# Token sums of a gated mixture layer computed in pieces during the attention, first two quads interleaved with the last attention batch

## The reference, cut to what matters

```
x = x + tanh(g_xattn) * attention(layernorm(x), ctx)       # 8 batches of 256 tokens, D = 512
h = layernorm(x)                                            # 2048 tokens
w_e  = top-8 of softmax(h @ gate_w.T), zeros elsewhere      # 64 experts
flat = w_e[:, inv_map]                                      # 8 groups of 8
soft = softmax over each group where flat != 0
scalar = flat.sum(-1)                                       # one per token and group
xg = h + soft @ mask_up[g]                                  # for each group g
a  = silu(xg @ gate[g].T) * (xg @ up[g].T)                  # 352 inner rows
x  = x + tanh(g_ffn) * sum_g scalar_g * (a @ down[g].T)
```

## Time and profile before

| What | Value |
|---|---|
| Median of 3 runs | 1113.91 us (1113.6 to 1114.71) |
| The profiled execution | 1112.23 us |
| Its span, first to last instruction | 1110.4 us |
| Mean granted TensorE clock | 0.983 |
| TensorE busy | 1056.9 us, 5388 matmuls |
| VectorE, ACT, GpSimd busy | 764.2, 376.9, 615.2 us |
| HBM read, written | 70.67 MB, 23.27 MB |

### The profile page before, as it was taken

One profiled execution on the slowest core, in us unless ns is written; L12 is line 12 of the kernel. 1 busy time (PEld: TensorE's weight loads), 2 busy tenths in 40 slices (PEclk: granted clock), 3 DMA queues, 4 the chain that ended last, 5 costly groups with the idle time before them and its releaser, 6 DMA issues.

```text
span 1110.4 us, 14594 instructions
## 1 busy us (share of the span) xinstructions
PE 1056.9 (95%) x5388; PEld 899.3 (81%) x5388; DVE 764.2 (69%) x1328; ACT 376.9 (34%) x635; POOL 615.2 (55%) x479
## 2 busy tenths in 40 slices
PE   8999999999977799989999999969999999999997
PEld 7988998998865677878888888858888888888885
DVE  7775666666588768797788787876656665666554
ACT  5333333333332344334234333333233333332331
POOL 1212201210344757765787876777777777777761
PEclk9999999999998899999999999989999999999999
DMA  9112213323682421113111211472222202221202
GB/s 331 59 39 95 63 61 86 82 79 48 125 264 102 89 65 54 64 43 66 53 64 44 71 65 62 141 228 93 99 72 71 71 28 71 72 71 46 71 27 76
DMA packets 86861, 94.75 MB, mean 85 GB/s; under 512 B 20240, under 2 KB 71184, under 8 KB 86800
## 3 DMA queue, kind: packets, MB, share of 16 engines
q1 hardware_dynamic: 86432, 93.80, 28.1%
q10 hardware_dynamic: 368, 0.15, 0.1%
HBM read 70.67 MB, written 23.27 MB: 85 GB/s over the span
## 4 chain that ended last, share of the span: by engine, by line
PE 85%; DVE 9%; DMA 2%; issue 2%; ACT 1%; SPq 1%; POOL 0%; POOLq 0%; DVEq 0%; ACTq 0%
PE bank L67 42%; PE bank L1500 35%; PE bank L1506 3%; PE bank L1514 2%; PE bank L1331 2%; DMA x_raw<-x 1%; DMA soft_stacks<-soft_out 1%; DMA w_raw<-in_w_qkvo 1%; DVE tmp L1302 1%; DVE x2t_lo L1175 0%; DVE soft L1026 0%; PE bank L1383 0%; DVE a_stack L1199 0%; SPq L426 0%; PE bank L1402 0%
## 5 line engine op out<-in xcount | busy, mean ns | idle before, releaser
L565 POOL TENSOR_TENSOR wgu_lo<-wgu_raw,wgu_hi 128x768 fp32r<-128x768 f32 (+1 forms) x132 | 208.9, 1590 | 196.4 <-ACT wgu_hi L756 196.4
L1500 PE MATMUL bank<-x2t_hi,wgu_lo 128*128 128x512 f32 x616 | 245.1, 398 | 30.7 <-DVE tmp L1273 9.7
L1500 PE MATMUL bank<-x2t_lo,wgu_hi 128*128 128x512 f32 x616 | 243.0, 395 | 0.0
L1500 PE MATMUL bank<-x2t_hi,wgu_hi 128*128 128x512 f32 x616 | 242.3, 393 | 0.0
L756 ACT CAST wgu_hi<-wgu_raw 128x768 fp32r<-128x768 f32 (+1 forms) x132 | 95.7, 727 | 262.2 <-PE bank L1506 205.4
L1500 PEld LDWEIGHTS bank<-x2t_hi,wgu_lo 128*128 128x128 f32 x616 | 117.6, 191 | 57.8 <-issue 27.6
L1217 DVE TENSOR_TENSOR xres<-xres,bank 128x512 f32<-128x512 f32 x176 | 120.1, 685 | 62.5 <-PE bank L67 62.5
L1500 PEld LDWEIGHTS bank<-x2t_hi,wgu_hi 128*128 128x128 f32 x616 | 117.6, 191 | 25.1
L67 PE MATMUL bank<-wd_hi,at_second 128*128 128x512 f32 x352 | 137.5, 391 | 0.0
L1500 PEld LDWEIGHTS bank<-x2t_lo,wgu_hi 128*128 128x128 f32 x616 | 117.8, 191 | 23.6
L67 PE MATMUL bank<-wd_hi,at_first 128*128 128x512 f32 x264 | 104.0, 394 | 9.1 <-issue 6.4
(11 more groups left out here) (194 smaller groups left out, 2294.7 us busy)
## 6 DMA issues: line engine op xcount, KB each, us to landing
wgu_raw<-in_w_gate_up SPq DMA_DIRECT2D x44, 512.0 KB, 3.8
wd_raw<-in_w_down SPq DMA_DIRECT2D x22, 512.0 KB, 4.9
a_stacks<-a_stack SPq DMA_DIRECT2D x22, 192.0 KB, 1.8
a_stack<-a_stacks SPq DMA_DIRECT2D x22, 192.0 KB, 3.7
ctxt_raw<-in_ctx_t SPq DMA_DIRECT2D x8, 512.0 KB, 11.4
ctx_raw<-in_ctx SPq DMA_DIRECT2D x8, 512.0 KB, 9.0
x<-x_raw SPq DMA_DIRECT2D x8, 512.0 KB, 4.0
w_raw<-in_w_qkvo SPq DMA_DIRECT2D x6, 512.0 KB, 7.7
```

The costliest lines, as they stand in the source:

```text
L565: nc.gpsimd.tensor_tensor(wgu_lo[:, group], wgu_raw[quad.set][:, group], f32(wgu_hi[:, group]), ALU.subtract).then_inc(s_fw_lo, 1)
L1500: last = nc.tensor.matmul(out_bank[:], stationary, moving, start=begins and n == 0, stop=n == len(pairs) - 1, skip_group_check=True)
```

## The change

The loops on the chip are written out (b = 0..7 on every engine). The token sums T1..T4 are no longer made between the halves. They are made in pieces of 128 token columns (`PIECES = 4` for each pass): SP loads the two halves of a piece of the whole x2 from HBM (512-byte runs), GpSimd makes the four sums in place (`piece_sums`), ACT the high part (`piece_high`), GpSimd (pass 1) or VectorE (pass 2) the low part (`piece_low`), and SP stores both in HBM. For pass 1 pieces 0 and 1 are loaded at the end of iteration 4 and worked in iteration 5, pieces 2 and 3 loaded at the end of iteration 5, into the same two buffers once pieces 0 and 1 are stored, and worked in iteration 6. For pass 2 one piece each is loaded in quads 11, 13, 15, 17 and worked in the quad after. The quads then load T1..T4 as ready high and low parts like the other blocks, seven blocks of 1 MB in the order in which the products read them. Quad 0's weights are loaded, summed and split in iteration 7, and its first blocks are loaded there too.

TensorE's order becomes: iteration 7 with `output(1)` ahead of the transposes of the probabilities, quad 0's first two products, `attend(7)`, and the rest of quad 0 interleaved with the transposes and outputs; quad 1's first two products come ahead of quad 0's last one. VectorE does the sums of a quad first and the routing steps after them. For quads 3 to 42 two downs stand before the product that needs SUM_3; for quads 0 to 2 and 43 all four at the end (`early_tiles`). GpSimd makes the weight sums ahead of the last low part of a quad. The last down weights have a buffer of their own.

```diff
-            load_raw(0, 0, x_raw[:, T1], 0, 0)
-            load_raw(0, 1, x_raw[:, T3], 0, 1)
...
             for b in range(B):
+                if b == B - 1:
+                    sp.wait_ge(s_piece_out, 32 * PIECES)
+                    load_weights(quads[0])
+                    sp.wait_ge(s_q, 2 * B)
+                    load_block(0, 0)
+                    load_block(0, 1)
                 if b >= 2:
                     store_x2(b - 2, ot_hi, ot_lo)
...
+                else:
+                    sp.wait_ge(s_k, 2 * B)
+                    load_block(0, 2)
+                    load_block(0, 3)
...
+                if b in (5, 6):
+                    store_piece(2 * (b - 5))
+                    store_piece(2 * (b - 5) + 1)
+                if b == 4:
+                    sp.wait_ge(s_mu_lo, 1)
+                if b in (4, 5):
+                    load_piece(2 * (b - 4))
+                    load_piece(2 * (b - 4) + 1)
...
+            def load_piece(i):
+                first, second, _ = piece_tokens(i)
+                if i >= PIECES:
+                    sp.wait_ge(s_piece_out, 32 * i)
+                elif i >= 2:
+                    sp.wait_ge(s_piece_out, 32 * 2)
+                sp.wait_ge(s_x2_raw_out, 16 * (second // S + 1))
+                for n, at in enumerate((first, second)):
+                    sp.dma_start(sums_raw[piece_home(i)][:, n], x2_dram[:, :, at:at + PIECE]).then_inc(s_piece_in[piece_home(i)], 16)
...
+            def store_piece(i):
+                _, _, at = piece_tokens(i)
+                sp.wait_ge(s_piece_lo, i + 1)
+                for dram, part in ((th_dram, sums_hi), (tl_dram, sums_lo)):
+                    sp.dma_start(dram[:, :, :, at:at + PIECE].rearrange("p t k n -> p (t k) n"),
+                                 f32(part[piece_home(i)][:]).rearrange("p c k n -> p (c k) n")).then_inc(s_piece_out, 16)
...
 (gpsimd)
+            for b in range(2, B):
+                pieces = (2 * (b - 5), 2 * (b - 5) + 1) if b in (5, 6) else ()
+                for i in pieces:
+                    piece_sums(i)
+                for i in pieces:
+                    piece_low(i)
+                if b == B - 1:
+                    weight_sums(quads[0])
+                    for n, group in enumerate((GROUP_A, GROUP_B, GROUP_C)):
+                        weight_low(quads[0], n, group)
+                x2_whole(b - 2, ot_hi, ot_lo)
+                context_lo(b)
...
 (scalar, iteration: after the high parts of q)
+                if b in (5, 6):
+                    piece_high(2 * (b - 5))
+                    piece_high(2 * (b - 5) + 1)
+                if not part.next:
+                    for n, group in enumerate((GROUP_A, GROUP_B, GROUP_C)):
+                        weight_high(quads[0], n, group)
                 key_hi(0)
...
 (tensor)
+            product_1(quad)
+            product_6(quad)
+            attend(B - 1)
+            masked_products(quad)
+            product_2(quad)
+            product_5(quad)
+            pe.wait_ge(s_o_lo, NT)
+            pe.wait_ge(s_xn2, NT - 2)
+            transposes(xn, 4, s_x2)
+            product_7(quad)
+            for t in range(ST):
+                output(t, first=6)
+            soft_products(quad)
+            product_4(quad)
+            product_1(after)
+            product_6(after)
+            product_3(quad)
+            pe.wait_ge(s_x1, NT)
+            logits(B - 2, *late_tokens())
+            product_2(after)
+            masked_products(after)
+            product_5(after)
+            product_7(after)
+            soft_products(after)
+            pe.wait_ge(s_logit_sb, B - 1)
+            pe.wait_ge(s_xn2, NT)
+            transposes(xn, 6, s_x2)
+            product_4(after)
+            product_3(after)
+            pe.wait_ge(s_x2_lo, NT)
+            logit_folds(7)
+            logits(B - 1, *late_tokens())
...
 (sync, quad 21)
+                    for order, read in enumerate((s_m1, s_m6, s_m2)):
+                        sp.wait_ge(read, q + 1)
+                        load_block(1, order + 1)
                     sp.wait_ge(s_act, 2 * q)
                     load_scalars(1, 0)
+                    for order, read in enumerate((s_m5, s_m7, s_m4)):
+                        sp.wait_ge(read, q + 1)
+                        load_block(1, order + 4)
...
 (scalar, down_weights)
-                if u >= 1:
+                if 1 <= u < UNITS - 1:
                     eng.wait_ge(s_down, UNIT_TILES * u)
```

More of the change, by code:

```diff
@@ L747, in _ @@
                         nc.scalar.copy(mu[:, :, :, copied], mu_raw[:]).then_inc(s_mu_hi, 1)
-            with eng.Fori(*LOOP) as b:
-                iteration(b, Parts())
-            iteration(B - 1, Parts(B - 1))
-            def group_a(quad):
-                return GROUP_A if quad.first_pass else GROUP_A_LATER
-            def weight_high(quad, n, group):
-                nc.scalar.copy(wgu_hi[:, group], wgu_raw[quad.set][:, group]).then_inc(s_fw_hi, 1)
-            def sum_high(s, n, which):
-                eng.wait_ge(s_t_raw, 4 * s + n)
-                nc.scalar.copy(x2t_hi[:, which], x_raw[:, which]).then_inc(s_t_hi, 1)
             def act_high(quad, c):
@@ L1474, in iteration @@
                     flat_products()
-                if part.back and part.next:
+                if part.back:
                     output(1)
@@ L1481, in iteration @@
                 transposes(probs, 6, s_pt)
-                if not part.next:
-                    output(1)
             pe.wait_ge(s_ident, 1)
@@ new lines, in _ @@
+            quad, after = quads[0], quads[1]
+            product_1(quad)
[13 more added lines that the diff above has]
+            product_1(after)
@@ L1631, in _ @@
-                soft_product(psum_a, quad, GATE, 0).then_inc(s_c11, 1)
-                if q == 1:
-                    pe.wait_ge(s_logit_sb, B - 1)
-                    pe.wait_ge(s_xn2, NT)
-                    transposes(xn, 6, s_x2)
-                if q >= 3:
-                    down(below)
-                    if q == 4:
+                product_2(quad)
+                product_5(quad)
+                product_7(quad)
+                soft_products(quad)
+                for n in range(early):
+                    if n == 1 and q == 4:
```

602 lines of the change are left out of this document (317 added, 285 removed).

## The result

The changed kernel takes 1097.99 us (median of 4 runs, 1097.01 to 1099.27) beside 1113.76 us of the kernel before (4 runs): a ratio of 0.9855, interval 0.9842 to 0.9869. It is faster by 15.8 us, and 26 us slower than the forecast of 1072; it lies outside the range of 1058 to 1086. Two executions in all the series, one of the kernel before (2027 us) and one of an experiment (1166 us), fell into a slower state of the chip and are left out of every comparison. The profiled execution took 1099.27 us around a span of 1097.5, 12.9 us less than before's 1110.4. All that follows is measured against that 12.9.

What follows compares the result with a forecast made beforehand. TensorE is busy for 1056.9 of 1110.4 us, so only its idle and half-clock time can be won. Terms -28 - 5 - 11.5 - 5.7 + 9 = -41 gave 1071 us profiled, 1072 us as median; range 1058 to 1086.

Steps and rivals of the forecast that it cites:

- Attention, +9: Attention iterations 5 to 7: waits for pieces, half clock and held routing steps cost 9 us, bounds 0 and +20.
- The 1.7 us of half clock: Iteration 6: the clock falls behind TensorE's 3 us pause at the logits, costing 1.7 us more.
- the 1 us at iteration 7's logits: Iteration 7: the same order of events makes ACT about 2 us late, and 1 us is lost.
- The reason given for the stacks: Routing chains, iterations 5 to 7: GpSimd's pauses let most VectorE steps through, so only 3.4 us are lost.
- Between the halves, -28: From 304 us to quad 3's start: pauses filled, 65 us instead of 93, 28 us less, bounds -34 to -19.
- The four waits that I had: Quads 0 to 2: product 5 of quad 1, logits copy, quad 2's first down and SUM_3; 6 us in all.
- Routing behind the sums, -5: Between 420 and 505 us: with sums first, routing delays only what has slack; 5 us less, bounds -7 to 0.
- Pieces of pass 2 under the slack they have: Four quads: GpSimd's 4 x 0.74 us and about 1 us of ACT and VectorE a quad cost nothing.
- The transfers hide: Pass boundary, 720 to 750 us: seven blocks' loads, 7 MB in 25 us, hide; 11.5 us less, bounds -12 to -6.
- The end, -5.7: Last downs: the 4.6 us pause and half clock go, 0.5 us wait for SUM_3 comes; -5.7 us, bounds -6.5 to -3.
- Quads 24 to 43, 0: Pass 2 after the boundary: forecast no difference, 0 us.
- The wait moves instead of going: Rival, 0.22: iterations 6 and 7 lose 15 to 20 us, or quads 0 to 2 keep 15 us of waits; 1078 to 1090.

Runs made afterwards that it cites:

- the kernel of 1084.04 us: The changed kernel with VectorE's route_scalars of batch 5 back in quad 2, behind route_groups: 1084.04 us, ratio 0.9744.
- from SyncE's side: The changed kernel with SyncE's store of batch 5's scalars in quad 3, behind the issue of quad 5's weights: 1085.60 us.
- the new buffer alone: The kernel before with only the last down weights' own buffers, ACT taking their high parts in quad 43 ahead of its last copies: 1106.96 us.
- two more small edits: Added to scalars in quad 2 and blocks first: pass 2 pieces' low parts before VectorE's product 7 wait, quad 0's low parts behind the context's: 1075.85 us.
- with the low parts last: Changed kernel, route_scalars of batch 5 in quad 2, GpSimd's low parts of quad 0's weights behind the context's in iteration 7: 1082.51 us.

## Why the forecast missed

The sum itself comes to 1072.7 (1113.91 - 41.2), written down as 1072.

**Attention, +9: right in size, and in part by luck, for errors cancel.** Measured 8.8 in this trace, but 6.2 to 8.8 in the eight traces with the same attention. Stores of the pieces, then loads, on SyncE:

```profile
217.94 0.52 SPq L460 DMA_DIRECT2D token_sums_h<-sums_hi  x1
...
233.67 2.59 SPq L454 DMA_DIRECT2D sums_raw<-x  x4
```

Loads at 233 were forecast; 233.67 it was, in a trace whose iteration 5 ends 2.1 us later than before's. Two terms were off against each other. The context load ahead took 10.1 us in place of 9.0 and landed at 227.65; it stood behind an 8 KB store of scalars, issued at 211.03 and landed at 223.59. The four stores then took 6.0 us to 233.66, and not 7.8: they land 1.5 us apart, 0.52 MB each, about 350 GB/s against my 270. The DMA view of 217.4 to 233.7 us has both, in 40 slices:

```profile
GB/s 60 50 30 50 10 50 10 20 40 30 10 10 30 10 60 70 256 417 370 397 415 382 376 351 341 348 348 347 344 349 348 346 343 351 348 343 263 172 87 0
```

By the Trainium skill's "DMA: Bandwidth & Descriptors" (Specifications) the line rate starts at 512 B, with 435 GB/s at the fabric and about 358 as one core's limit at HBM. These stores of 512-byte rows do not reach the first figure, which the prediction took from there; they agree with the second. ACT then:

```profile
244.09 1.05 ACT L800 CAST sums_hi<-sums_raw 128x1024 fp32r<-128x1024 f32 x1 [2.11 <-POOL sums_raw L667]
245.04 0.58 ACT L751 CAST kt_hi<-bank 128x512 fp32r<-128x512 f32 x1
```

TensorE waited 2.2 us at the logits of iteration 6 (forecast 3) and 0.8, 1.3, 2.0 us for the stacks in iterations 5 to 7 (forecast 0.3, 1.2, 1.9). The 1.7 us of half clock came, 1.6 of them, but in iteration 7 and not behind the logits of iteration 6, where the granted clock is 1.00; the 1 us at iteration 7's logits did not come. The reason given for the stacks (GpSimd's pauses let most steps through) was not the whole: see the last section.

**Between the halves, -28: measured -23.8, inside its bounds.** The four waits that I had are there: 0.9 us at `a_tmp` in quad 1 (forecast 1), 1.6 at the logits (2), 2.4 at the first down (2), 0.6 at SUM_3 (1). Two more came in quad 2, 0.8 for `a_tmp` and 1.3 for `a_stack`, so the rest is 7.6 us and not 6. The clock stays at 1.00 there. The other 2.6 us of the difference were not told apart.

**Routing behind the sums, -5: the step that failed.** "The routing delays only what has a quad's length of slack" and "the delay is absorbed" looked at who reads the routing's result on TensorE. It did not look at SyncE, which waits for the scalars in program order with quad 5's weights behind. The place behind the sums is not at fault, since the kernel of 1084.04 us keeps it; the move of `route_scalars` to the next quad is. It cost 11.3 us of wait and some 1.5 of half clock, 12.8 us of the stage in the trace; undoing that one step gives 14.0 us by the medians, and from SyncE's side 12.4. Without it the -5 holds: quads 5 to 12 gave -5.1, and quads 3 to 5 take 34.6 us for before's 35.6. This one omission is near half of the miss of 28 us; without it the time lies inside the range, at 1084.04.

**"Pieces of pass 2 under the slack they have", 0: wrong by 5.6 us**, of which their removal gives 4.9. I compared 3 us of GpSimd a quad with the average idle time. But their place in GpSimd's and VectorE's lists delays what is queued behind them, and each GpSimd sum can hold a two-input step of VectorE (last section).

**"The transfers hide", -11.5: measured -7.5.** The bytes did fit; I took a rate and not the order. The scalar rows stood ahead of the last three blocks. With the blocks first, quads 21 to 24 take 48.9 us for before's 60.8, so -11.9 was to be had.

**The end, -5.7: right**, -5.1 in the trace; the new buffer alone gives 5.3.

**Quads 24 to 43, 0: +1.4 us**, 303.0 for 301.6, and 303.0 in every trace with the change. It is no wait. The six matmuls of product 1 in pass 2 read their tokens from `x2t_spare`, a buffer that the change adds, and they follow each other more slowly:

```profile
842.80 0.40 PE L1605 MATMUL bank<-x2t_spare,wgu_lo 128*128 128x512 f32 x1
...
844.21 0.39 PE L1605 MATMUL bank<-x2t,wgu_lo 128*128 128x512 f32 x1
```

Here six take 1.41 us from start to start, where 6 x 0.227 would be 1.36. Each of the 114 such matmuls in these quads is followed by the next after 230 to 236 ns, 233.8 in the mean; before, no product matmul there was followed after more than 227. That is 0.8 of the 1.4 us, and the rest lies with some of the matmuls around them. Why they are slower was not tested.

Of the rivals none was what happened. "The wait moves instead of going" named the attention and quads 0 to 2; the wait came at quad 4, by a list I had not walked through. With the scalars and the blocks back in a good order and two more small edits the kernel takes 1075.85 us, 4 us above the forecast of 1072.

## What to carry to other kernels

When a step is moved later, ask every engine's list who waits for its result, the issuing engine of the DMAs first: there a wait for a small store holds every load behind it. Work "under the slack" must be placed, not averaged: what counts is what is queued behind it. And on a full queue a transfer that nobody needs yet goes behind those that someone waits for.

## What the runs showed of the hardware

**A small store on a shared queue.** I had not expected that an 8 KB store, made of 4-byte elements, holds what is issued behind it on the same queue. It takes 12.7 us to land, and the 512 KB weight load behind it lands 1.6 to 1.7 us after it, whenever it was issued: 409.51 behind 407.90 in the changed kernel (13.0 us from its issue), 386.11 behind 384.40 with the scalars in quad 2 (10.8), 406.99 behind 405.29 with the store a quad later (9.6). The same load takes 4.2 us in the median, also when it is issued ahead of that store. From 394 to 412 us the queue moved 1.45 MB in 3024 packets, 2128 of them under 512 B.

**Which VectorE steps GpSimd holds.** Not a share of all steps: the kind of step decides. All executions of four lines of the changed kernel (ns: least, median, most):

```profile
L1137 DVE TENSOR_TENSOR soft<-soft,flat x8: 291/726/2389, 128.4 to 582.5; 128x128 f32<-128x128 f32 x8
```
```profile
L1138 DVE TENSOR_REDUCE grp_max<-soft x8: 285/286/290, 128.7 to 583.3; 128x16 f32<-128x128 f32 x8
```
```profile
L1297 DVE TENSOR_TENSOR tmp<-tmp,scalars x88: 691/1113/1834, 345.5 to 1082.9; 128x512 f32<-128x512 f32 x88
```
```profile
L1304 DVE TENSOR_TENSOR xres<-xres,bank x176: 671/686/689, 379.0 to 1094.3; 128x512 f32<-128x512 f32 x176
```

Two-input steps with both operands in SBUF are stretched up to the length of a GpSimd operation (2.4 us), and so is the TENSOR_SCALAR in the rows above; the reduction never, and the sum with a PSUM bank as one input never, in 176 executions. The Trainium skill's "SBUF — State Buffer" (Who interferes with whom) says just this, and the trace agrees: two SBUF inputs or a two-port mode contend with GpSimd, a reduction does not, and the later one waits for the whole instruction. Read with that, the held steps of the attention can be counted: at most one for each GpSimd operation that runs beside such steps. In the rows above three operations hold three steps, and in iteration 7 with the low parts last two hold two. The scalars' product L1297 took 693 ns in the median before (L1210) and 1113 now; with GpSimd's old order it is 1110 and without the pieces of pass 2 1113, so neither of these edits explains why more of its executions collide.
